# First loads of the attention stage moved into the last projection batch, queries stored in pieces there, output weights rounded one round later

## The chip, the cores and the metric

The kernel runs on one core of a Trainium2 chip. The metric is the device time of one execution in microseconds (us): the kernel before took 1955.43 us as the median of 3 runs, between 1955.02 and 1957.78. All times inside an execution come from one profiled execution. TensorE is called PE below, VectorE DVE, ScalarE ACT, GpSimd POOL; SP is the sync engine, which here only issues DMAs.

## The reference

Eight sequences of 512 tokens with 512 features go through one block: cross attention (16 heads of 32 features, with an additive bias for each head and a mask for each sequence) and a feed-forward part with a routed low-rank branch. Cut to what matters here:

```
q = split(layernorm(x) @ Wq.T + bq);  k = split(ctx @ Wk.T + bk);  v = split(ctx @ Wv.T + bv)
scores = q @ k^T / sqrt(32)
scores = where(mask == 0, -1e9, scores) + attn_bias          # bias: 16 heads x 512 x 512
probs = softmax(scores);  x = x + (probs @ v) @ Wo.T + bo
x = x + gelu(z @ W1.T) @ W2.T + routed low-rank term of z,   z = layernorm(x)
```

Everything is float32. Products that need it are made from a high and a low part of each operand ("rounding" a weight below means making these two parts).

## The kernel before, in words

The program has three blocks that follow each other, with a barrier of all engines between them; the first, `project`, ends only when all its DMAs to DRAM have landed.

`project` walks over the 8 sequences (batches). For each it computes keys, values and queries, in this order, and stores them to DRAM (`k_d`, `v_d`, `q_d`), with the mask turned into an additive array `pos_d`. Beside that it loads, splits and stores an eighth of the feed-forward weights (`load_ff`, `store_ff`, to `wf_d`). All DMAs of this block are issued by SP in program order, each behind the wait that stands before it. In a batch: `load_ff`, next context and x, store of the keys, store of `pos`, next mask, four stores of the values, one store of the queries (1 MB, after DVE has written the fourth query tile, L353), then `store_ff` (four DMAs of 512 KB).

`attend` has 8 rounds. A round is one group of 4 heads with 4 sequences: 16 steps, called quads here (a quad is 128 query rows of one sequence, with 4 heads; 128 quads in all, 16 in a round, counted from 0). For each head of a quad:
- PE multiplies queries by keys into PSUM (L651);
- POOL writes `pos - bias` into the buffer `t_s` (L619, 128x512). There are four buffers, so POOL may be up to four quads ahead. Six of the 64 tiles in a round are made by DVE instead (L727);
- DVE adds the two and takes the row minimum (L742); ACT takes the exponential (L797); PE turns the tile (L662), ACT and DVE copy it out (L784, L749), and PE multiplies by the values (L676).

At the start SP loads, for the first sequence, `pos`, queries, keys and values (`load_pos`, `load_qk`, `load_v`, 2.75 MB with the first bias rows), then waits for the fourth bias DMA before it goes on with the other three sequences. POOL issues the bias rows: `bias_t` holds four parts of 1 MB, for query rows `qt` 0 to 3; part 0 at once, parts 1 to 3 after the first queries and keys are there. Every second round POOL issues the next head group's four bias parts, one after each of its last four quads.

The output weights `Wo` are loaded in the first round and rounded there: ACT makes the high part at step `GQ` of round 0 (quad 4, L807), DVE the low part at step `GQ + 2` (quad 6, L773).

`blend` then does the output projection and the feed-forward part, and is the longest block.

## Time and profile before

| | |
|---|---|
| median of 3 runs | 1955.43 us |
| the profiled execution, its own time | 1953.16 us |
| its span, from first to last instruction | 1951.4 us |
| granted PE clock, mean | 0.979 of full |
| busy: PE, DVE, ACT, POOL | 1829.2, 1034.6, 794.3, 885.4 us |
| `project` | 0 to 318.3 us |
| `attend` | 318.9 to 935.8 us |
| `blend` | the rest |

The profile gives for each engine how long it was busy, and for a wait how long the engine sat idle and what ended that. The span is divided by the two barriers into the three blocks; a block has its own bound, and an average over the span says little on any of them. PE counts as busy while matmuls are in its pipeline.

### The profile page before, as it was taken

Reading aid. Unit: us, or ns where it says so; the run is one execution under the profiler, and the core shown is the slowest. Engines: PE = TensorE matmul, PEld = TensorE weight load, DVE = VectorE, ACT = ScalarE, POOL = GpSimd, SP = SyncE. Lnnn points to the kernel's source line nnn. Section 1 sums busy time; section 2 is a strip of 40 time slices with the busy share of each in tenths; the row PEclk is TensorE's granted clock in tenths of the full one; section 3 lists DMA queues with packets and bytes.
Section 4 is the critical chain, followed back from the end, with each engine's and each line's share of the span. In section 5 each row is a group of like instructions: output and inputs, shape, how many; then the busy total and the mean of one; then the engine's idle time right before and its main releaser. Section 6 shows DMA issues by size and latency. Waiting matters only on the chain.

```text
span 1951.4 us, 31562 instructions
## 1 busy us (share of the span) xinstructions
PE 1829.2 (94%) x11736; PEld 1363.2 (70%) x11736; DVE 1034.6 (53%) x2402; ACT 794.3 (41%) x1720; POOL 885.4 (45%) x705
## 2 busy tenths in 40 slices
...
GB/s 285 257 304 301 268 292 215 255 109 196 131 108 190 138 107 179 150 120 12 147 100 108 152 183 130 172 181 154 183 130 175 181 161 173 130 183 179 137 193 117
DMA packets 196359, 335.91 MB, mean 172 GB/s; under 512 B 10352, under 2 KB 51952, under 8 KB 196208
## 3 DMA queue, kind: packets, MB, share of 16 engines
...
q14 instruction: 55, 0.45, 0.1%
...
## 4 chain that ended last, share of the span: by engine, by line
PE 41%; DVE 5%; ACT 4%; issue 1%; DVEq 0%; POOL 0%; ACTq 0%
PE n_ps_h L1379 15%; PE n_ps_y L1398 14%; PE n_ps_m L1315 9%; PE n_ps_y L1315 2%; PE n_ps_m L1309 1%; DVE n_w L1087 1%; ACT n_g_f L1269 1%; DVE n_sel L1096 1%; DVE n_hl L1110 1%; ACT L1269 1%; ACT L1253 1%; ACT L1250 1%; DVE n_w L1091 1%; DVE n_w L1084 0%; ACT n_u L1250 0%
## 5 line engine op out<-in xcount | busy, mean ns | idle before, releaser
L619 POOL TENSOR_TENSOR a_t_s<-a_pos,a_bias_t 128x512 f32<-128x512 f32 x464 | 576.1, 1275 | 3.4 <-PE a_ps_t L662 3.1
L996 POOL TENSOR_TENSOR n_g_l<-n_g_f,n_g_h 128x512 fp32r<-128x512 f32 x128 | 184.3, 1440 | 676.4 <-DVE n_g_h L1169 676.4
L797 ACT ACTIVATE a_t_s<-a_t_s,a_nmax 128x512 f32<-128x512 f32 x512 | 364.3, 715 | 36.2 <-DVE a_nmax L742 36.0
L1379 PE MATMUL n_ps_h<-n_zT_h,n_w 128*128 128x512 f32 x1024 | 343.4, 397 | 2.1 <-DVE n_r_row L1145 2.1
L742 DVE CUSTOM_DVE_ANT_0 a_t_s<-a_ps_s,a_t_s 128x512 f32<-128x512 f32 x464 | 294.0, 687 | 64.1 <-PE a_ps_s L651 30.7
L1169 DVE CAST n_g_h<-n_g_f 128x512 fp32r<-128x512 f32 x128 | 54.6, 427 | 514.4 <-ACT n_g_f L1269 514.4
L662 PEld LDWEIGHTS a_ps_t<-ident,a_t_s 128*128 128x128 f32 x2048 | 222.0, 142 | 142.8 <-issue 108.8
L1398 PE MATMUL n_ps_y<-n_w,n_g_h 128*128 128x512 f32 x1024 | 316.2, 390 | 0.0
L1269 ACT ACTIVATE n_g_f<-n_ps_h 128x512 f32<-128x512 f32 x128 | 75.6, 596 | 547.3 <-PE n_ps_h L1379 547.3
L662 PE MATMUL a_ps_t<-ident,a_t_s 128*128 128x128 f32 x2048 | 282.4, 282 | 6.1 <-ACT a_pT L784 6.1
L1379 PEld LDWEIGHTS n_ps_h<-n_zT_h,n_w 128*128 128x128 f32 x1024 | 196.0, 191 | 43.3 <-DVE n_r_row L1145 2.5
L1398 PEld LDWEIGHTS n_ps_y<-n_w,n_g_h 128*128 128x128 f32 x1024 | 191.8, 188 | 39.4
L1379 PE MATMUL n_ps_h<-n_zT_l,n_w 128*128 128x512 f32 x512 | 202.4, 395 | 0.0
L1398 PE MATMUL n_ps_y<-n_w,n_g_l 128*128 128x512 f32 x512 | 199.5, 390 | 0.0
L784 ACT ACTIVATE a_pT<-a_ps_t 128x512 f32<-128x512 f32 x256 | 151.5, 592 | 74.0 <-PE a_ps_t L662 73.9
L651 PE MATMUL a_ps_s<-a_k,a_q 32*128 32x512 f32 x1024 | 148.4, 649 | 31.3 <-DMA a_k<-k_d 19.9
L749 DVE COPY a_pT<-a_ps_t 128x512 f32<-128x512 f32 x256 | 164.5, 683 | 7.0 <-PE a_ps_t L662 7.0
L676 PE MATMUL a_ps_o<-a_pT,a_v 128*32 128x256 f32 x2048 | 150.8, 390 | 0.0
L282 POOL TENSOR_TENSOR p_wf_l<-p_wf,p_wf_h 128x2048 fp32r<-128x2048 f32 x8 | 37.0, 4622 | 185.4 <-ACT p_wf_h L393 185.4
L1379 PEld LDWEIGHTS n_ps_h<-n_zT_l,n_w 128*128 128x128 f32 x512 | 98.1, 192 | 20.1
L1398 PEld LDWEIGHTS n_ps_y<-n_w,n_g_l 128*128 128x128 f32 x512 | 96.1, 188 | 19.9
L651 PEld LDWEIGHTS a_ps_s<-a_k,a_q 32*128 32x128 f32 x1024 | 41.4, 186 | 87.7 <-DVE a_nmax L742 46.9
...
## 6 DMA issues: line engine op xcount, KB each, us to landing
n_w<-wf_d SPq DMA_DIRECT2D x256, 512.0 KB, 4.0
a_pos<-pos_d SPq DMA_DIRECT2D x32, 1024.0 KB, 5.9
a_bias_t<-in_bias POOLq DMA_DIRECT2D x16, 1024.0 KB, 6.7
p_c_raw<-in_ctxT SPq DMA_DIRECT2D x8, 1024.0 KB, 7.5
p_x_raw<-in_x SPq DMA_DIRECT2D x8, 1024.0 KB, 9.7
p_m_raw<-in_mask SPq DMA_DIRECT2D x8, 1024.0 KB, 12.1
k_d<-p_k_s SPq DMA_DIRECT2D x8, 1024.0 KB, 11.6
pos_d<-p_pos SPq DMA_DIRECT2D x8, 1024.0 KB, 9.9
```

The source lines that it names most:

```text
L619: pool.tensor_tensor(out=t_s[:, j % NN, i, :], in0=pos[:, b, qt, :], in1=bias_t[:, i, qt, :], op=ALU.subtract).then_inc(nbm_pool, 1)
L651: pe.matmul(ps_s[:, i, :], q[rows, b, qt * P:(qt + 1) * P], k[rows, b, :], start=True, stop=True).then_inc(scored, 1)
L662: last = pe.transpose(ps_t[:, BANK[i], kt * P:(kt + 1) * P], t_s[:, at[1] % NN, i, kt * P:(kt + 1) * P], ident[:, :])
L676: last = pe.matmul(ps_o[rows, :], v[:, b, kt, rows], pT[:, h, i, kt, :], start=kt == 0, stop=kt == NT - 1)
L742: dve.tensor_tensor_reduce(t_s[:, j % NN, i, :], ps_s[:, i, :], added, 1.0, 3.0e38, ALU.add, ALU.min, nmax[:, j % NN, i:i + 1]).then_inc(s ...
L749: dve.tensor_copy(dst, src).then_inc(kept_dve, 1)
L784: act.activation(dst, src, ACT.Copy).then_inc(kept_act, 1)
L797: act.activation(t_s[:, j % NN, i, :], t_s[:, j % NN, i, :], ACT.Exp, scale=-1.0, bias=nmax[:, j % NN, i:i + 1], accum_out=total[:, j // 2 ...
L996: pool.tensor_tensor(out=g_l[:, f % NG, :], in0=g_f[:, f % NG, :], in1=g_h[:, f % NG, :].bitcast(F32), op=ALU.subtract).then_inc(g_low, 1)
L1315: last = pe.matmul(dst, stationary, moving, start=start and n == 0, stop=stop and n == len(passes) - 1)
L1379: last = pe.matmul(ps_h[:, f % 2, :], stationary, moving, start=i == 0, stop=i == len(passes) - 1)
L1398: last = pe.matmul(ps_y[:, t, :], gs[i], w2[:, f % NW, j, :], start=f == 0 and m == 0 and isinstance(b, int) and b == 0, stop=f == NF - 1 ...
```

## The change

It does four things.

1. Queries and keys of the first four sequences (`q`, `k`), the first sequence's `pos` and bias part 0 get their own SBUF space (`Ahead`) outside the blocks. In the last projection batch, behind `load_ff`, SP loads them there (`load_ahead`, ten DMAs, 4 MB). `attend` starts with them in place: SP then issues only `v` and `pos`, and POOL issues bias parts 1 to 3 with no wait between.
2. In the last batch the queries are stored in four pieces, each as soon as DVE has written its tile, with `store_ff` between the second and the third.
3. `Wo` is rounded at steps `GQ` and `GQ + 2` of round 1 instead of round 0.
4. `blend` takes the space of `Ahead` for its tiles `g_f`, `rc`, `hl`, `sel`, `u`, `w` and `ln_w`.

Its core:

```diff
+            def load_ahead():
+                sp.wait_ge(pos_out, 16 * 2)
+                sp.dma_start(ahead.pos[:, :, :], tokens(pos_d[0])).then_inc(ahead.pos_in, 16)
+                sp.dma_start(ahead.bias[:, :, :], bias[0, 0:HG, 0:P, :].rearrange("h p n -> p h n")) \
+                    .then_inc(ahead.bias_in, 16)
+                sp.wait_ge(q_out, 16 * (NT + 1))
+                sp.wait_ge(k_out, 16 * (NT + 1))
+                for n in range(NT):
+                    sp.dma_start(ahead.q[:, n, :], q_d[n]).then_inc(ahead.qk_in[n], 16)
+                    sp.dma_start(ahead.k[:, n, :], k_d[n]).then_inc(ahead.qk_in[n], 16)
             def body(b, more):
                 sp.wait_ge(wf_low, b + 1)
                 load_ff(b)
+                if not more:
+                    load_ahead()
...
-                sp.wait_ge(bank_free, NPB + NVQ * (b + 1))
-                store_qk(b, q_s, q_d, q_out)
-                sp.wait_ge(wf_low, b + 2)
-                store_ff(b)
+                if more:
+                    sp.wait_ge(bank_free, NPB + NVQ * (b + 1))
+                    store_qk(b, q_s, q_d, q_out)
+                else:
+                    for c in range(NC):
+                        if c == NC // 2:
+                            sp.wait_ge(wf_low, b + 2)
+                            store_ff(b)
+                        sp.wait_ge(bank_free, NPB + NVQ * b + NT + c + 1)
+                        sp.dma_start(q_d[B * c + b], q_s[:, c, :]).then_inc(q_out, 16)
+                if more:
+                    sp.wait_ge(wf_low, b + 2)
+                    store_ff(b)
...
-            load_pos(0, 0)
-            load_qk(0, 0)
             load_v(0, 0)
+            load_pos(0, 1)
+            load_v(0, 1)
             sp.wait_ge(bias_in[NT - 1], 16)
-            for j in range(1, NG):
+            for j in range(2, NG):
                 load_pos(0, j)
-                load_qk(0, j)
                 load_v(0, j)
...
-            load_bias(0, 0)
-            pool.wait_ge(qk_in[0], 32)
             for qt in range(1, NT):
                 load_bias(0, qt)
...
-                if isinstance(g, int) and g == 0 and j == GQ + 2:
+                if g == 1 and j == GQ + 2:
                     dve.wait_ge(kept.wo_high, 1)
...
-                if isinstance(g, int) and g == 0 and j == GQ:
+                if g == 1 and j == GQ:
                     act.wait_ge(kept.wo_in, 16)
...
-        g_f = sb("g_f", [P, NG, S])
+        g_f = ahead.pos
...
-        rc, hl, sel = sb("rc", [P, NT, NB]), sb("hl", [P, NT, NB]), sb("sel", [P, NT, NB])
-        u, w, ln_w = sb("u", [P, NT, NB]), sb("w", [P, NT, NB]), sb("ln_w", [P, NT, NB])
+        rc, hl, sel, u, w, ln_w = (a[:, n:n + 2, :].rearrange("p a (b n) -> p (a b) n", n=NB)
+                                   for a in (ahead.q, ahead.k, ahead.bias) for n in (0, 2))
```

SP's rows of the last projection batch, before (`p_wf` are the feed-forward weights as loaded, `p_wf_h` and `p_wf_l` their two parts; a DMA row ends with its shape):

```order
124 L216 DMA p_wf<-in_W1T 128x4x128
125 L218 DMA p_wf<-in_W2T 128x512
126 L212 DMA k_d<-p_k_s 128x4x512 [waits p_k_done]
127 L236 DMA pos_d<-p_pos 128x4x512 [waits p_pos_done]
128 L241 DMA v_d<-p_v_s 128x4x128 [waits p_bank_free]
129 L241 DMA v_d<-p_v_s 128x4x128 x3
130 L212 DMA q_d<-p_q_s 128x4x512 [waits p_bank_free]
131 L222 DMA wf_d<-p_wf_h 128x1024 [waits p_wf_low]
132 L223 DMA wf_d<-p_wf_l 128x1024
133 L222 DMA wf_d<-p_wf_h 128x1024
134 L223 DMA wf_d<-p_wf_l 128x1024
```

and the same place in the changed kernel, from the last row of `load_ff` to the keys' store (`h_` names are those of `Ahead`), and then from the values' store on:

```order
125 L232 DMA p_wf<-in_W2T 128x512
126 L241 DMA h_pos<-pos_d 128x4x512 [waits p_pos_out]
127 L242 DMA h_bias<-in_bias 128x4x512
128 L247 DMA h_q<-q_d 128x512 [waits p_k_out,p_q_out]
129 L248 DMA h_k<-k_d 128x512
134 L247 DMA h_q<-q_d 128x512
135 L248 DMA h_k<-k_d 128x512
136 L226 DMA k_d<-p_k_s 128x4x512 [waits p_k_done]
```

```order
139 L268 DMA v_d<-p_v_s 128x4x128 x3
140 L278 DMA q_d<-p_q_s 128x512 [waits p_bank_free] x2
141 L236 DMA wf_d<-p_wf_h 128x1024 [waits p_wf_low]
142 L237 DMA wf_d<-p_wf_l 128x1024
143 L236 DMA wf_d<-p_wf_h 128x1024
144 L237 DMA wf_d<-p_wf_l 128x1024
145 L278 DMA q_d<-p_q_s 128x512 [waits p_bank_free] x2
```

Ten loads now stand between `load_ff` and the store of the keys (rows 130 to 133 are two more pairs of `h_q` and `h_k`), and half of the queries leaves before `store_ff`, half behind it.

POOL's rows at the start of `attend`, before (`a_bias_t` is the bias, `a_t_s` what POOL writes):

```order
29 L606 DMA a_bias_t<-in_bias 128x4x512
30 L606 DMA a_bias_t<-in_bias 128x4x512 [waits a_qk_in0]
31 L606 DMA a_bias_t<-in_bias 128x4x512 x2
32 L619 TENSOR_TENSOR a_t_s<-a_pos,a_bias_t 128x512 [waits a_turned,a_bias_in0,a_pos_in0]
33 L619 TENSOR_TENSOR a_t_s<-a_pos,a_bias_t 128x512 [waits a_turned] x3
34 L619 TENSOR_TENSOR a_t_s<-a_pos,a_bias_t 128x512 [waits a_turned,a_bias_in1]
```

and in the changed kernel:

```order
29 L656 DMA a_bias_t<-in_bias 128x4x512 x3
30 L669 TENSOR_TENSOR a_t_s<-h_pos,h_bias 128x512 [waits a_turned,h_bias_in,h_pos_in]
31 L669 TENSOR_TENSOR a_t_s<-h_pos,h_bias 128x512 [waits a_turned] x3
32 L669 TENSOR_TENSOR a_t_s<-h_pos,a_bias_t 128x512 [waits a_turned,a_bias_in1]
33 L669 TENSOR_TENSOR a_t_s<-h_pos,a_bias_t 128x512 [waits a_turned] x2
```

One bias DMA and the wait for the first queries and keys are gone ahead of POOL's first tile; the tile's own shape is as it was.

## Rows read from the trace of the kernel before

**Rows 1.** Busy time by window around the last projection batch (columns as headed).

```profile
core 0: us, PE busy (x) PEld busy (x) DVE busy (x) ACT busy (x) POOL busy (x), PEclk, DMA share, GB/s
272.70:292.70 20.00, 19.32 (x94) 16.07 (x93) 13.11 (x27) 4.82 (x8) 1.01 (x1) 1.00 0.90 315
292.70:297.10 4.40, 4.40 (x26) 3.78 (x25) 1.39 (x2) 0.00 (x0) 0.00 (x0) 1.00 0.00 0
297.10:302.20 5.10, 5.10 (x25) 4.21 (x24) 0.75 (x1) 2.40 (x2) 2.43 (x1) 1.00 0.73 206
302.20:309.00 6.80, 5.96 (x27) 4.61 (x25) 2.25 (x3) 0.00 (x0) 2.18 (x1) 1.00 0.00 0
309.00:318.30 9.30, 0.00 (x0) 0.00 (x0) 0.00 (x0) 0.00 (x0) 0.00 (x0) 0.60 0.87 338
```

**Rows 2.** SP's DMA issues by time: start, duration, tile, count.

```profile
312.30 1.27 SPq L223 DMA_DIRECT2D wf_d<-p_wf_l  x1
...
318.91 0.37 SPq L542 DMA_DIRECT2D a_pos<-pos_d  x1
```

**Rows 3.** POOL by time: start, duration, count, idle time before and its releaser.

```profile
319.31 0.92 POOL L606 DMA_DIRECT2D a_bias_t<-in_bias  x1 [14.93 <-POOLq L119]
328.31 2.23 POOL L606 DMA_DIRECT2D a_bias_t<-in_bias  x3 [8.08 <-DMA a_k<-k_d]
330.56 39.40 POOL L619 TENSOR_TENSOR a_t_s<-a_pos,a_bias_t 128x512 f32<-128x512 f32 x32
...
374.43 6.49 POOL L619 TENSOR_TENSOR a_t_s<-a_pos,a_bias_t 128x512 f32<-128x512 f32 x4 [0.49 <-PE a_ps_t L662]
...
779.33 4.98 POOL L619 TENSOR_TENSOR a_t_s<-a_pos,a_bias_t 128x512 f32<-128x512 f32 x4
```

**Rows 4.** DVE by time, the same columns.

```profile
332.01 0.69 DVE L742 CUSTOM_DVE_ANT_0 a_t_s<-a_ps_s,a_t_s 128x512 f32<-128x512 f32 x1 [23.06 <-POOL a_t_s L619]
...
373.75 2.33 DVE L773 TENSOR_TENSOR k_wo_l<-k_az,k_wo_h 128x2048 fp32r<-128x2048 f32 x1
...
785.75 0.69 DVE L742 CUSTOM_DVE_ANT_0 a_t_s<-a_ps_s,a_t_s 128x512 f32<-128x512 f32 x1
```

**Rows 5.** ACT by time, at quad 4.

```profile
361.64 1.91 ACT L807 ACTIVATE k_wo_h<-k_az 128x2048 fp32r<-128x2048 f32 x1 [4.80 <-DMA k_az<-in_WoT]
```

**Rows 6.** PE by time, quads 0, 5, 8, 9 and 12 (L651).

```profile
328.06 2.09 PE L651 MATMUL a_ps_s<-a_k,a_q 32*128 32x512 f32 x8 [19.89 <-DMA a_k<-k_d]
...
355.44 1.14 PE L651 MATMUL a_ps_s<-a_k,a_q 32*128 32x512 f32 x8
...
379.62 1.14 PE L651 MATMUL a_ps_s<-a_k,a_q 32*128 32x512 f32 x8
...
383.87 1.14 PE L651 MATMUL a_ps_s<-a_k,a_q 32*128 32x512 f32 x8
...
398.01 1.14 PE L651 MATMUL a_ps_s<-a_k,a_q 32*128 32x512 f32 x8
```

**Rows 7.** The page's group of POOL's tiles: busy, mean ns, idle before, releaser.

```profile
L619 POOL TENSOR_TENSOR a_t_s<-a_pos,a_bias_t 128x512 f32<-128x512 f32 x464 | 576.1, 1275 | 3.4 <-PE a_ps_t L662 3.1
```

**Rows 8.** Waits in 318 to 930: total us, times, longest us.

```profile
DVE a_t_s L742 <- POOL a_t_s L619: 27.3, 13, 23.1
```

**Rows 9.** Busy time by window at the start of `attend` (columns as in rows 1).

```profile
322.00:326.00 4.00, 0.00 (x0) 0.00 (x0) 0.00 (x0) 0.00 (x0) 0.00 (x0) 0.50 1.00 373
...
334.00:338.00 4.00, 1.58 (x8) 0.52 (x8) 1.40 (x4) 2.40 (x6) 4.00 (x5) 0.50 1.04 394
```

**Rows 10.** DMA issues one by one: KB, us from issue to landing.

```profile
q_d<-p_q_s SPq DMA_DIRECT2D x1, 1024.0 KB, 4.2
...
wf_d<-p_wf_l SPq DMA_DIRECT2D x1, 512.0 KB, 6.0
...
a_pos<-pos_d SPq DMA_DIRECT2D x1, 1024.0 KB, 5.7
a_bias_t<-in_bias POOLq DMA_DIRECT2D x1, 1024.0 KB, 9.5
```

More of the change, by code:

```diff
@@ L56, in build, with __init__, sb @@
         neg_half = top.enter_context(nc.sbuf_tensor("neg_half", [P, NT], F32))
+        ahead = Ahead(nc, top)
         project(nc, ident, ones, neg_half, x, ctxT, mask, WqT, bq, WkT, bk, WvT, bv, W1T, W2T,
-                q_d, k_d, v_d, pos_d, wf_d)
+                q_d, k_d, v_d, pos_d, wf_d, bias, ahead)
         kept = Kept(nc, top)
-        attend(nc, ident, bias, q_d, k_d, v_d, pos_d, att_d, x, WoT, bo, rawU, rawV, kept)
-        blend(nc, ident, ones, neg_half, x, att_d, ln_g, ln_b, rWT, rb, gamma, wf_d, kept, out)
+        attend(nc, ident, bias, q_d, k_d, v_d, pos_d, att_d, x, WoT, bo, rawU, rawV, kept, ahead)
+        blend(nc, ident, ones, neg_half, x, att_d, ln_g, ln_b, rWT, rb, gamma, wf_d, kept, ahead, out)
+class Ahead:
+    def __init__(self, nc, stack):
+        def sb(name, shape):
+            return stack.enter_context(nc.sbuf_tensor("h_" + name, shape, F32))
+        self.q, self.k = sb("q", [P, NT, S]), sb("k", [P, NT, S])
+        self.pos = sb("pos", [P, NT, S])
+        self.bias = sb("bias", [P, HG, S])
+        self.qk_in = [stack.enter_context(nc.semaphore(f"h_qk_in{n}")) for n in range(NT)]
+        self.pos_in, self.bias_in = (stack.enter_context(nc.semaphore("h_" + n)) for n in ("pos_in", "bias_in"))
 class Kept:
@@ L114, in project @@
 def project(nc, ident, ones, neg_half, x, ctxT, mask, WqT, bq, WkT, bk, WvT, bv, W1T, W2T,
-            q_d, k_d, v_d, pos_d, wf_d):
+            q_d, k_d, v_d, pos_d, wf_d, bias, ahead):
     NPJ = 3 * NC
@@ L259, in _ @@
             sp.wait_ge(k_out, 16 * (B + 1))
-            sp.wait_ge(q_out, 16 * (B + 1))
+            sp.wait_ge(q_out, 16 * (B + NC))
             sp.wait_ge(v_out, 16 * NC * (B + 1))
@@ L449, in _, with attend @@
             walk(pe, body)
-def attend(nc, ident, bias, q_d, k_d, v_d, pos_d, att_d, x, WoT, bo, rawU, rawV, kept):
+def attend(nc, ident, bias, q_d, k_d, v_d, pos_d, att_d, x, WoT, bo, rawU, rawV, kept, ahead):
     NG = 4
@@ L471, in sem @@
             return ctx.enter_context(nc.semaphore("a_" + name))
-        q, k = sb("q", [P, NG, S]), sb("k", [P, NG, S])
+        q, k = ahead.q, ahead.k
         v = sb("v", [P, NG, NT, P])
-        pos = sb("pos", [P, NG, NT, S])
-        bias_t = sb("bias_t", [P, HG, NT, S])
+        pos_more = sb("pos", [P, NG - 1, NT, S])
+        bias_more = sb("bias_t", [P, HG, NT - 1, S])
         t_s = sb("t_s", [P, NN, HG, S])
@@ L487, in attend @@
         ps_o = ctx.enter_context(nc.psum_tensor("a_ps_o", [P, HALF], F32))
-        qk_in = [sem(f"qk_in{n}") for n in range(NG)]
+        qk_in = ahead.qk_in
         v_in = [sem(f"v_in{n}") for n in range(NG)]
-        pos_in = [sem(f"pos_in{n}") for n in range(NG)]
+        pos_in = [ahead.pos_in] + [sem(f"pos_in{n}") for n in range(1, NG)]
         bias_in = [sem(f"bias_in{t}") for t in range(NT)]
@@ L499, in attend, with pos_rows, bias_rows, wait_bias @@
         passed = sem("passed")
+        def pos_rows(j, qt, end):
+            return ahead.pos[:, qt:end, :] if j == 0 else pos_more[:, j - 1, qt:end, :]
+        def bias_rows(i, end, qt):
+            return ahead.bias[:, i:end, :] if qt == 0 else bias_more[:, i:end, qt - 1, :]
+        def wait_bias(eng, hg, qt):
+            if qt == 0 and hg == 0:
+                eng.wait_ge(ahead.bias_in, 16)
+            else:
+                eng.wait_ge(bias_in[qt], 16 * (hg + (qt > 0)))
         def lagged(g, j, lag):
@@ L541, in load_pos @@
             def load_pos(g, j):
-                sp.dma_start(pos[:, j, :, :], tokens(pos_d[g % (B // NG) * NG + j])).then_inc(pos_in[j], 16)
+                sp.dma_start(pos_rows(j, 0, NT), tokens(pos_d[g % (B // NG) * NG + j])).then_inc(pos_in[j], 16)
             def load_qk(g, j):
@@ L605, in load_bias @@
                 rows = slice(qt * P, (qt + 1) * P)
-                pool.dma_start(bias_t[:, :, qt, :], bias[0, hg * HG:(hg + 1) * HG, rows, :].rearrange("h p n -> p h n")) \
+                pool.dma_start(bias_rows(0, HG, qt), bias[0, hg * HG:(hg + 1) * HG, rows, :].rearrange("h p n -> p h n")) \
                     .then_inc(bias_in[qt], 16)
```

17 lines of the change are left out of this document (8 added, 9 removed).

## The prediction, made before the result was known

> **What bounds the kernel now.** I read the windows first, since the change sits at one barrier. The last projection batch runs from about 272 us, and SP's queue has holes in it: DMA share 0.90, then 0.00 for 4.4 us, 0.73 while the values leave, 0.00 for 6.8 us, and then 0.87 for 9.3 us in which no engine computes [rows 1]. That last stretch is the store of the queries and of the feed-forward weights: the last DMA is issued at 312.30 and lands 6.0 us later, at 318.3 [rows 2, 10]. `attend` starts at 318.91 with its loads [rows 2].
>
> Then the queues by time. PE sits idle for 19.89 us, until the first keys are there at 328.06 [rows 6]; only then POOL issues three bias DMAs, 2.23 us, and starts its first tile at 330.56. DVE starts at 332.01, after 23.06 us idle, released by POOL [rows 3, 4]. So the first tile of `attend` hangs on POOL, and POOL on the first keys.
>
> What bounds the rest of `attend` decides what an earlier start is worth. Two chains run side by side. POOL's 464 tiles are busy 576.1 us and idle only 3.4, 3.1 of it for PE [rows 7]: POOL practically never stops. But DVE waits for POOL only 13 times, 27.3 us in all, 23.1 of it at the start [rows 8]: behind the start POOL is nearly always ahead, and the chain PE-DVE-ACT sets the pace. So there are two limits close together. How close, I read at the worst place, the first quad of the last head group (quad 96), just behind POOL's four bias issues: POOL's four tiles end at 779.33 + 4.98 = 784.31 [rows 3], and DVE takes the fourth of them at 785.75 [rows 4]. POOL's lead is down to 1.4 us there. POOL loses time to bias issues at the end of each head group and makes it up on the way; behind quad 96 it loses none any more.
>
> The stall that the third edit is about: in round 0 ACT waits 4.80 us for `Wo` and computes 1.91 us [rows 5], and DVE spends 2.33 us [rows 4]. Quads 5 to 8 start 24.18 us apart, quads 9 to 12, the same three steps undisturbed, 14.14 [rows 6]. The chain loses 10.0 us. POOL hardly does: it runs through with 32 tiles in 39.40 us [rows 3].
>
> **The change part by part.** *End of `project`.* Ten loads, 4 MB (4.19 million bytes), join SP's queue. At the full pace of loads, 373 to 394 GB/s [rows 9], they take 10.6 to 11.2 us; I take 10.8. They stand behind `load_ff`, and what comes later in the queue (keys, `pos`, values, queries, `store_ff`) is pushed back into the holes, which are 4.4 + 6.8 = 11.2 us [rows 1]. Nobody waits for those stores before the barrier. Where the queue no longer runs dry, its two restarts go as well: a lone 1 MB store takes 4.2 us to land [rows 10] for 2.7 us of transfer at that pace, 1.5 us each time, 3.0 for two. So the queue ends earlier by 11.2 + 3.0 - 10.8 = 3.4 us, at 314.9. Bounds: the bytes of 272.7 to 318.3 (20 us at 315, 5.1 at 206, 9.3 at 338 GB/s: 10.5 million) plus 4.2 make 14.7; at 338 GB/s from 272.7 they end at 316.2, 2.1 us earlier than now. On the other side the fourth query piece cannot be issued before 309.0 [rows 1], and with the 6.0 us of a DMA in a full queue [rows 10] it lands at 315.0, or at 313.2 with the 4.2 of a lone one: at best 5.1 us. The splitting of the queries alone has no term: they share the queue with `store_ff`, whose wait, for POOL's 4.6 us on the weights, is over early in the window of 302.2 to 309.0: POOL is busy 2.18 us of it [rows 1].
>
> *Start of `attend`.* SP and POOL begin 0.6 us behind the landing, at 315.5 and 315.9. POOL issues its three bias DMAs (2.23 us) and starts its first tile at 315.9 + 2.25 = 318.15, where it stood at 330.56: 12.4 us earlier. Of this 3.4 is the queue's and 9.0 the wait for `q` and `k`. DVE follows 1.45 us later, as now (332.01 - 330.56). The first tile's data are there by then: `pos`, bias, `q` and `k` stand in the queue ahead of seven stores that must land before the barrier.
>
> *What is late next:* bias part 1. POOL needs it for its fifth tile, 4 x 1.24 us (39.40 / 32) behind the first, at 323.1. Now a bias part issued together with SP's loads takes 9.5 us, while SP's `pos` of the same size takes 5.7 [rows 10]. It landed when nearly all of the 2.75 MB was through; in the changed kernel 2.5 MB are ahead of or beside it, so 9.5 x 2.5 / 2.75 = 8.6 us, at 324.5. POOL stalls 1.4 us. Bounds: 0 (with 5.7) and 2.3 (with 9.5). Parts 2 and 3 follow at 2.7 us each, faster than the 3.7 to 5 us in which POOL uses one up.
>
> The Trainium skill says otherwise on that wait: by "DMA: Bandwidth & Descriptors", section "Queues, rings and completion order", each DMA engine takes turns between its queues packet by packet. Two equal transfers would then end together; the rows have 5.7 and 9.5 us, so here the measurement decides. By the rule part 1 would be there after about 7.7 us, at 323.6, and the stall would be 0.5 instead of 1.4.
>
> *`Wo` one round later.* The wait of 4.80 us goes, since `Wo` is loaded long before; 1.91 us on ACT and 2.33 on DVE stay, in round 1. The chain gains 10.0 less between 0 and 4.2; I take 3.3 (all of DVE's, as the nearer engine to the limit, and half of ACT's): 6.7. POOL gains its idle time for PE, 3.1 us [rows 7], since the chain is no longer four quads behind. One loss stays POOL's in both kernels: beside DVE's 2.33 us four tiles took 6.49 instead of 4.98 [rows 3], 1.5 us.
>
> "SBUF — State Buffer" of the Trainium skill, section "Who interferes with whom", lets a DVE operation with two SBUF inputs block POOL for its whole length. The rows show 1.5 of 2.33 us; if the new place made it all of it, POOL would lose 0.8 us more.
>
> *`blend`'s tiles and the views of `pos` and bias* change addresses, not shapes: nothing, bounded by nothing that a row shows.
>
> **The sum.** The chain alone would end `attend` 12.4 + 6.7 = 19.1 us earlier. But POOL must have quad 96's tiles ready: 784.31 - 330.56 - 3.1 = 450.65 us of POOL's work behind its first tile, so at 318.15 + 1.4 + 450.65 = 770.2. DVE can take the fourth at 770.2 instead of 785.75: 15.5 us earlier. It is the smaller of the two, and behind quad 96 the chain keeps its pace. So 12.4 (start) + 3.1 (POOL's waits) + 1.4 (its lead) - 1.4 (bias part 1) = 15.5 us. `blend` shifts by it whole. From the profiled execution's 1953.16 us that leaves 1937.7; the median of the runs is 2.3 us above that execution, and I predict 1940 us as the next median.
>
> **The rivals.** *A: the chain is the limit to the end*, because POOL makes up the missing 4 us (its idle time was more than the profile shows, or bias part 1 is in time). For it: DVE waits for POOL 4.2 us in all behind the start [rows 8]. Against it: 464 tiles at 1.24 us leave POOL no reserve. Gain 17 (POOL without the stall) to 19: 1937.
>
> *B: the queue does not end earlier.* The 4 MB only just fit the holes. If loads and stores mixed run at 315 GB/s (the mean of the first window [rows 1]), 14.7 million bytes take 46.7 us, to 319.4: 1.1 later than now. With the full 2.3 us stall the gain is 15.5 - 4.5 - 0.9 = 10: 1945.
>
> *C: no change.* The transfers were hidden behind something the profile does not name, for instance code that must be loaded at the barrier; or POOL's tiles beside more DMA traffic take longer. Then only what the chain can use is left, under 4 us: 1953.
>
> *D: slower.* The queue is the place: everything in `project` must land before the barrier, and ten loads are put ahead of it. Its price is set by the pace of the mixed queue. At 206 GB/s, the pace while the values leave [rows 1], 14.7 million bytes take 71 us, to 344: 26 us later than now, against which stand 9.0 + 3.1 + 1.4 - 1.4 = 12: 14 us slower, 1969. It decides at 318.3 + 12.1 = 330.4, 57.7 us of transfer or 255 GB/s. Against it: the first window holds 315, and the 206 is mostly the restart of a queue with 1 MB in it.
>
> **How the numbers follow.** Under 0.2%, 3.9 us, a measurement cannot tell this kernel from no change. Chances: the forecast 0.45, A 0.22, B 0.23, C 0.06, D 0.04. Faster by more than 0.2% are the first three, 0.90; within it 0.06; slower 0.04. The range takes in A with the queue at its best bound (15.5 + 1.7 + 1.4, and a little of the chain's) and B: 1935 to 1946.
>
> **What the profile after would show.** Right: the windows from 287 to 309 us with a DMA share near 0.9; the last landing at 313 to 316; PE's first scores within 1 us of the barrier, POOL's first tile 2.7 us behind it; one POOL wait of 1 to 2 us before its fifth tile; no ACT wait for `Wo`, and PE's quads 5 to 8 in 14 us; DVE waits for POOL late in each head group, more than now; and POOL's tiles without a gap. Wrong: a last landing behind 318 (B or D), DVE that still never waits for POOL (A), POOL tiles over 1.3 us, or a `blend` that is longer than before.

## The result and the profile after

| | before | after |
|---|---|---|
| median | 1955.43 us (13 runs, 1952.08 to 1959.76) | 1948.85 us (13 runs, 1943.87 to 1950.81) |
| ratio, with its 95% interval | | 0.9961 [0.9952, 0.9969] |
| profiled execution, its span | 1951.4 us | 1947.8 us |
| first scores of `attend` (PE) | 328.06 us | 317.06 us |
| scores of the last quad (127) | 925.01 us | 919.14 us |

The changed kernel is faster, by 6.6 us in the medians. The forecast was 15.5 us less than before, 1940 us, with a range to 1946: the sign was right, the size was not, and the time lies outside the range.

The two profiled executions must be set against each other with care: in that of after, `project` runs 2.2 us late from its first 60 us on, before any instruction that the change touches (its last batch starts at 274.90 instead of 272.70). In the kernels below this shift is between nothing and 2.1 us (e3 2.0, e6 1.7, e7 1.8, e4 0.2), so I compare durations between two points of one execution where I can, and raw times where the shift does not matter.

The windows around the last projection batch, the same columns as in [rows 1] and the stretches 2 to 3 us later, with a sixth window from round 1 of `attend`:

```profile
274.90:294.90 20.00, 19.32 (x94) 16.01 (x93) 13.14 (x27) 4.81 (x8) 1.01 (x1) 1.00 0.99 344
294.90:299.30 4.40, 4.40 (x26) 3.78 (x24) 1.33 (x2) 0.00 (x0) 0.00 (x0) 1.00 1.05 387
299.30:305.00 5.70, 5.70 (x27) 4.73 (x27) 0.81 (x2) 2.40 (x2) 2.97 (x1) 1.00 1.06 396
305.00:311.00 6.00, 5.43 (x24) 4.15 (x23) 2.03 (x3) 0.00 (x0) 1.65 (x1) 1.00 1.09 397
311.00:316.30 5.30, 0.00 (x0) 0.00 (x0) 0.22 (x1) 0.00 (x0) 0.00 (x0) 0.83 0.70 279
427.00:441.00 14.00, 4.10 (x40) 2.19 (x32) 14.00 (x12) 3.93 (x11) 11.76 (x10) 0.75 0.00 1
```

The holes of [rows 1] are full: share 0.00, 0.73 and 0.00 became 1.05, 1.06 and 1.09, at 387 to 397 GB/s. The stretch in which no engine computes has shrunk from 9.3 to 5.3 us. The sixth window is the trouble: DVE busy for 14 us of 14, and no DMA at all.

SP's issues by time (start, duration, tile, count), the last pieces of the queries and the first load of `attend`, against [rows 2]:

```profile
309.71 2.44 SPq L278 DMA_DIRECT2D q_d<-p_q_s  x2
317.01 0.37 SPq L600 DMA_DIRECT2D a_v<-v_d  x1
```

POOL by time (start, duration, count, idle time before and its releaser), against [rows 3]:

```profile
317.40 2.42 POOL L656 DMA_DIRECT2D a_bias_t<-in_bias  x3 [10.75 <-POOLq L133]
319.83 4.93 POOL L669 TENSOR_TENSOR a_t_s<-h_pos,h_bias 128x512 f32<-128x512 f32 x4
326.25 6.19 POOL L669 TENSOR_TENSOR a_t_s<-h_pos,a_bias_t 128x512 f32<-128x512 f32 x5 [1.48 <-DMA a_bias_t<-in_bias]
...
427.69 4.97 POOL L669 TENSOR_TENSOR a_t_s<-a_pos,h_bias 128x512 f32<-128x512 f32 x4
432.63 6.13 POOL L669 TENSOR_TENSOR a_t_s<-a_pos,a_bias_t 128x512 f32<-128x512 f32 x5
443.88 2.50 POOL L669 TENSOR_TENSOR a_t_s<-a_pos,a_bias_t 128x512 f32<-128x512 f32 x2 [5.12 <-PE a_ps_t L710]
...
773.44 4.98 POOL L669 TENSOR_TENSOR a_t_s<-h_pos,h_bias 128x512 f32<-128x512 f32 x4
```

The first tile stands at 319.83 instead of 330.56, and the one wait for bias part 1 is there, 1.48 us. At 438.76 POOL has no buffer left and waits 5.12 us for PE.

DVE by time, against [rows 4]:

```profile
321.29 0.69 DVE L789 CUSTOM_DVE_ANT_0 a_t_s<-a_ps_s,a_t_s 128x512 f32<-128x512 f32 x1 [10.07 <-POOL a_t_s L669]
...
430.06 10.85 DVE L820 TENSOR_TENSOR k_wo_l<-k_az,k_wo_h 128x2048 fp32r<-128x2048 f32 x1
440.83 0.68 DVE L789 CUSTOM_DVE_ANT_0 a_t_s<-a_ps_s,a_t_s 128x512 f32<-128x512 f32 x1
...
779.88 0.69 DVE L789 CUSTOM_DVE_ANT_0 a_t_s<-a_ps_s,a_t_s 128x512 f32<-128x512 f32 x1
```

The line of 10.85 us decides the case. The same operation on the same tile, the low part of `Wo`, took 2.33 us before [rows 4] and takes 10.85 now. Everything behind it on DVE waits, and then PE does.

PE by time, quads 0, 5 and 8, then 23 and 24 with what PE does just ahead of 24, against [rows 6]:

```profile
317.06 2.09 PE L699 MATMUL a_ps_s<-h_k,h_q 32*128 32x512 f32 x8 [6.63 <-PEq L133]
...
345.65 1.14 PE L699 MATMUL a_ps_s<-h_k,h_q 32*128 32x512 f32 x8
...
359.78 1.14 PE L699 MATMUL a_ps_s<-h_k,h_q 32*128 32x512 f32 x8
...
428.93 1.14 PE L699 MATMUL a_ps_s<-h_k,h_q 32*128 32x512 f32 x8
...
441.67 1.08 PE L733 MATMUL a_ps_s<-ident,a_rinv 128*32 128x128 f32 x16 [10.57 <-DVE a_nmax L789]
...
446.44 1.71 PE L699 MATMUL a_ps_s<-h_k,h_q 32*128 32x512 f32 x8
```

Quads 5 to 8 are 14.13 us apart, where they were 24.18. Quads 23 and 24 are 17.51 apart, where they were 4.96; PE has idled 10.57 us for DVE, and its granted clock was 0.50 of full (1.2 GHz) from 441 to 446 us and 1.00 again from 452 on (in the kernel before it was 1.00 from 436 to 460). Set against the scores of before, PE is 11.0 us earlier at quad 0, 19.84 from quad 8 to 21, 6.44 at quad 24 (452.88 before), and 5.87 from quad 25 to the end. The gain was there and went in one step.

ACT at the high part of `Wo`, against [rows 5]: no wait is left.

```profile
420.21 1.91 ACT L854 ACTIVATE k_wo_h<-k_az 128x2048 fp32r<-128x2048 f32 x1
```

The waits from 318 to 930 us (engine, what it waited for: total us, times, longest), against [rows 7, 8]:

```profile
DVE a_t_s L789 <- POOL a_t_s L669: 14.1, 12, 10.1
...
POOL a_t_s L669 <- PE a_ps_t L710: 8.1, 3, 5.1
...
POOL a_t_s L669 <- DMA a_bias_t<-in_bias: 1.5, 1, 1.5
```

POOL's waits for PE were to vanish from 3.1 us; they are 8.1 (5.12, 2.45 and 0.56), all behind DVE's long operation.

### The profile page after: what moved, and what is told of

Read it like the earlier page. It is cut to its first block, busy times and chain, and to the rows that moved or that the text cites. A ratio compares the mean times of both kernels' runs of the same rounds, so it can differ in the third digit from the quotient of the medians.

```text
span 1947.8 us, 31566 instructions
## 1 busy us (share of the span) xinstructions
PE 1834.0 (94%) x11736; PEld 1365.9 (70%) x11736; DVE 1043.5 (54%) x2402; ACT 794.6 (41%) x1720; POOL 882.9 (45%) x704
## 4 chain that ended last, share of the span: by engine, by line
PE 42%; DVE 5%; ACT 4%; issue 1%; DVEq 0%; POOL 0%; ACTq 0%
PE n_ps_h L1426 15%; PE n_ps_y L1445 14%; PE n_ps_m L1362 9%; PE n_ps_y L1362 2%; PE n_ps_m L1356 1%; DVE h_bias L1134 1%; ACT h_pos L1316 1%; DVE h_k L1143 1%; DVE h_q L1157 1%; ACT L1316 1%; ACT L1300 1%; ACT L1297 1%; DVE h_bias L1138 1%; DVE h_bias L1131 0%; ACT h_k L1297 0%
## 5 line engine op out<-in xcount | busy, mean ns | idle before, releaser
L1043 POOL TENSOR_TENSOR n_g_l<-h_pos,n_g_h 128x512 fp32r<-128x512 f32 x128 | 184.2, 1439 | 680.9 <-DVE n_g_h L1216 680.9
L1216 DVE CAST n_g_h<-h_pos 128x512 fp32r<-128x512 f32 x128 | 54.6, 426 | 516.3 <-ACT h_pos L1316 516.3
L669 POOL TENSOR_TENSOR a_t_s<-a_pos,a_bias_t 128x512 f32<-128x512 f32 x256 | 317.7, 1271 | 7.8 <-PE a_ps_t L710 7.6
L1316 ACT ACTIVATE h_pos<-n_ps_h 128x512 f32<-128x512 f32 x128 | 75.6, 596 | 548.2 <-PE n_ps_h L1426 548.1
L699 PE MATMUL a_ps_s<-h_k,h_q 32*128 32x512 f32 x1024 | 148.4, 649 | 18.9 <-DVE a_nmax L789 8.4
L669 POOL TENSOR_TENSOR a_t_s<-a_pos,h_bias 128x512 f32<-128x512 f32 x96 | 119.6, 1270 | 0.6 <-PE a_ps_t L710 0.6
```

Of the source, the lines that this page charges most:

```text
L669: pool.tensor_tensor(out=t_s[:, j % NN, i:i + 1, :], in0=pos_rows(b, qt, qt + 1), in1=bias_rows(i, i + 1, qt), op=ALU.subtract).then_inc(n ...
L699: pe.matmul(ps_s[:, i, :], q[rows, b, qt * P:(qt + 1) * P], k[rows, b, :], start=True, stop=True).then_inc(scored, 1)
L1043: pool.tensor_tensor(out=g_l[:, f % NG, :], in0=g_f[:, f % NG, :], in1=g_h[:, f % NG, :].bitcast(F32), op=ALU.subtract).then_inc(g_low, 1)
```

## The experiments

All of them were timed against the kernel before, whose medians beside them were 1955.44 to 1956.28 us; each experiment has 4 to 12 executions. One of the twelve of e2_only_wo_round1 took 2330.37 us, the others 1952.91 to 1965.78, and its median counts all twelve. The next table gathers them; "from scores to scores" is the time from the first scores of `attend` to those of quad 127 in the profiled execution, which is free of the shift in `project`; the low part is the time of the operation (or the piece of it) that the row moves.

| kernel | median us | ratio [95%] | first scores | quad 127 | from scores to scores | low part of `Wo` |
|---|---|---|---|---|---|---|
| before | 1955.43 | 1 | 328.06 | 925.01 | 596.95 | DVE 2.33 |
| after | 1948.85 | 0.9961 [0.9952, 0.9969] | 317.06 | 919.14 | 602.08 | DVE 10.85 |
| e1_wo_round0 | 1948.21 | 0.9961 [0.9946, 0.9976] | 317.04 | 920.57 | 603.53 | DVE 12.33 |
| e2_only_wo_round1 | 1959.96 | 1.0013 [1.0, 1.0026] | 328.59 | 927.81 | 599.22 | DVE 10.11 |
| e3_wo_low_pool_end | 1938.35 | 0.9907 [0.9891, 0.9923] | 316.89 | 909.54 | 592.65 | POOL 4.55 |
| e4_reduce_in_place | 1939.01 | 0.9911 [0.9896, 0.9926] | 315.10 | 908.43 | 593.33 | as e3 |
| e5_pool_pause | 1942.89 | 0.994 [0.9928, 0.9953] | 316.12 | 914.63 | 598.51 | DVE 2.28 |
| e6_bias_first | 1935.22 | 0.9893 [0.988, 0.9907] | 316.75 | 907.48 | 590.73 | as e3 |
| e7_no_pieces | 1942.53 | 0.9939 [0.9926, 0.9951] | 320.80 | 913.29 | 592.49 | as e3 |
| e8_low_in_pieces | 1944.73 | 0.9945 [0.9931, 0.9958] | 314.75 | 914.65 | 599.90 | DVE 9.28 (first quarter) |
| e9_seventh_tile | 1938.82 | 0.9911 [0.9895, 0.9926] | 316.33 | 909.66 | 593.33 | as e3 |

The rest of the program, from quad 127's scores on, takes 1025.4 to 1030.4 us in these profiled executions, 1026.4 in that of before and 1028.7 in that of after. The change touches it only by the addresses of `blend`'s tiles (its part 4), e3 and its successors by when the first attention output is loaded. Kernels with the same `blend` differ by as much as before and after do, so the 2.3 us between these two are not shown to be the change's; why it varies was not tried.

The theory: DVE's subtraction of `Wo` reads two tiles in SBUF, as nothing else that DVE does at this place (the tiles that it takes over from POOL are no exception: there DVE subtracts the bias from the scores where they lie, in PSUM); while POOL's tiles run one behind the other, it does not get on, and it ends only when POOL stops. The first rival: the place in round 1 is at fault (a transfer, the PE clock, the order around quad 22), and in round 0 the operation would take its 2.33 us. The second: the operation is long and dear in itself wherever DVE has it.

**e1_wo_round0** puts the rounding back to round 0 of the changed kernel.

```diff
-                if g == 1 and j == GQ + 2:
+                if g == 0 and j == GQ + 2:
...
-                if g == 1 and j == GQ:
+                if g == 0 and j == GQ:
```

> The changed kernel with Wo rounded in round 0 again (part 3 of the change undone). Theory 1: DVE's low part of Wo (two SBUF inputs) cannot start while POOL's tiles run back to back; it gets its turn only when POOL pauses, and POOL pauses only when it is four quads ahead. At quad 6 POOL is 1 to 3 quads ahead, so the operation should again take 8 to 13 us instead of 2.33, and the time be 1947 to 1951 us, as the changed kernel's. Theory 2: the operation is slow only where the change put it (round 1: other addresses, other neighbours); back in round 0 it takes 2.3 us as in the kernel before, and the time is 1940 to 1944 us.

DVE by time, at the low part of `Wo`:

```profile
356.95 12.33 DVE L820 TENSOR_TENSOR k_wo_l<-k_az,k_wo_h 128x2048 fp32r<-128x2048 f32 x1
```

POOL by time, beside it (the four tiles ahead of these are unbroken as well):

```profile
360.93 6.20 POOL L669 TENSOR_TENSOR a_t_s<-a_pos,a_bias_t 128x512 f32<-128x512 f32 x5
372.24 2.51 POOL L669 TENSOR_TENSOR a_t_s<-a_pos,a_bias_t 128x512 f32<-128x512 f32 x2 [5.11 <-PE a_ps_t L710]
```

POOL stops at 367.13, its tiles at 1.24 us each as ever, and DVE's operation ends at 369.28, 2.15 us later, about what it takes alone (2.28 us in e5 below). In the changed kernel the same difference is 440.91 - 438.76 = 2.15. It is not the round. The medians cannot tell this kernel from the changed one (1948.21 and 1948.85; from scores to scores it is 1.5 us longer): moving the rounding to round 1 is worth nothing that can be measured, for with the earlier loads ACT's wait of 4.80 us [rows 5] is gone in round 0 as well.

**e2_only_wo_round1** is the kernel before with the third part of the change alone.

```diff
-                if isinstance(g, int) and g == 0 and j == GQ + 2:
+                if g == 1 and j == GQ + 2:
...
-                if isinstance(g, int) and g == 0 and j == GQ:
+                if g == 1 and j == GQ:
```

> The kernel before with only part 3 of the change. Theory 1: without the wait for Wo in round 0 POOL's lead stays small, it never pauses, and the low part in round 1 takes 8 to 13 us; the 10 us won in round 0 are given back: 1953 to 1957 us, no change. Theory 2 in the form that the start of the attention stage (loads, buffers of Ahead) is the cause: the operation takes 2.3 us here, and the time is 1948 to 1950 us.

DVE by time:

```profile
440.40 10.11 DVE L773 TENSOR_TENSOR k_wo_l<-k_az,k_wo_h 128x2048 fp32r<-128x2048 f32 x1
```

POOL by time:

```profile
434.84 13.51 POOL L619 TENSOR_TENSOR a_t_s<-a_pos,a_bias_t 128x512 f32<-128x512 f32 x11
453.47 2.51 POOL L619 TENSOR_TENSOR a_t_s<-a_pos,a_bias_t 128x512 f32<-128x512 f32 x2 [5.12 <-PE a_ps_t L662]
```

Without the early loads it is the same: POOL stops at 448.35, DVE ends at 450.51, 2.16 us behind. The chain is 9.49 us ahead of before until quad 21, by the wait that goes, and 2.8 us behind it from quad 24. This part alone brings nothing or costs a little (1.0013 [1.0, 1.0026]).

Why was it cheap before? There POOL was about to stop, by chance. POOL and DVE by time in the kernel before, around 373.75 us:

```profile
370.17 3.77 POOL L619 TENSOR_TENSOR a_t_s<-a_pos,a_bias_t 128x512 f32<-128x512 f32 x3 [0.21 <-PE a_ps_t L662]
373.75 2.33 DVE L773 TENSOR_TENSOR k_wo_l<-k_az,k_wo_h 128x2048 fp32r<-128x2048 f32 x1
374.43 2.78 POOL L619 TENSOR_TENSOR a_t_s<-a_pos,a_bias_t 128x512 f32<-128x512 f32 x1 [0.49 <-PE a_ps_t L662]
```

The 4.80 us wait on ACT had put the chain so far behind that POOL ran out of buffers. DVE's operation started in the last of POOL's tiles, which ended at 373.94, and ended at 376.08, 2.14 us behind it: the same distance as in the other kernels. POOL's pause of 0.49 us let it in, and POOL's next tile took 2.78 us instead of 1.24 and ended 1.13 us behind DVE's end: this time POOL waited, for all that was left of DVE's operation. The stall that the change removes was what made the operation cheap.

**e3_wo_low_pool_end** takes the operation off DVE: POOL does it behind its last tile, where nobody waits for POOL. SP's load that needs it moves ahead of the last store.

```diff
             for j in range(NG):
+                if j == NG - 1:
+                    sp.wait_ge(kept.wo_low, 1)
...
+            pool.wait_ge(kept.wo_high, 1)
+            pool.tensor_tensor(out=kept.wo[1][:, :, :], in0=kept.az[:, :, :],
+                               in1=kept.wo[0][:, :, :].bitcast(F32), op=ALU.subtract).then_inc(kept.wo_low, 1)
...
-                if g == 1 and j == GQ + 2:
-                    dve.wait_ge(kept.wo_high, 1)
-                    dve.tensor_tensor(out=kept.wo[1][:, :, :], in0=kept.az[:, :, :],
-                                      in1=kept.wo[0][:, :, :].bitcast(F32), op=ALU.subtract).then_inc(kept.wo_low, 1)
```

> The changed kernel with the low part of Wo made by POOL behind its last tile of the attention stage instead of by DVE in round 1 (SP then loads the first attention output behind that). Theory 1: DVE is never held; the chain keeps its 19.8 us until POOL's lead becomes the limit, so the gain is that of POOL's start and lead, 13 to 15 us in the profile: 1940 to 1943 us. Theory 3 (the stall in round 1 only took the place of one that POOL's lead would have caused anyway): 1946 to 1950 us. POOL's own operation is expected at 4.6 us.

POOL by time: the start, quad 96, and the moved operation.

```profile
319.67 4.93 POOL L671 TENSOR_TENSOR a_t_s<-h_pos,h_bias 128x512 f32<-128x512 f32 x4
326.34 3.73 POOL L671 TENSOR_TENSOR a_t_s<-h_pos,a_bias_t 128x512 f32<-128x512 f32 x3 [1.75 <-DMA a_bias_t<-in_bias]
...
765.42 4.98 POOL L671 TENSOR_TENSOR a_t_s<-h_pos,h_bias 128x512 f32<-128x512 f32 x4
...
908.99 4.55 POOL L686 TENSOR_TENSOR k_wo_l<-k_az,k_wo_h 128x2048 fp32r<-128x2048 f32 x1
```

DVE by time, the third and fourth tile of quad 96:

```profile
769.35 0.69 DVE L794 CUSTOM_DVE_ANT_0 a_t_s<-a_ps_s,a_t_s 128x512 f32<-128x512 f32 x1 [0.53 <-issue]
770.58 0.69 DVE L794 CUSTOM_DVE_ANT_0 a_t_s<-a_ps_s,a_t_s 128x512 f32<-128x512 f32 x1 [0.54 <-issue]
```

The kernel is 17.1 us faster than before, two and a half times the gain of the change. Here the forecast's picture can be seen. The chain is ahead of before by 19.75 us behind round 0, and then by 18.9 at quad 24, 18.07 at quad 63, 16.58 at quad 95, 15.12 at quad 98, and 15.47 at quad 127: the gain is cut down at each new head group, behind POOL's bias issues. At quad 96 POOL's fourth tile ends at 765.42 + 4.98 = 770.40, and DVE takes it at 770.58. The lead of 1.4 us is 0.2, and the limit is POOL.

**e4_reduce_in_place** asks whether any DVE operation at that place is held. It is e3 with a reduction of the same 128x2048 tile put where the subtraction was; it reads one tile in SBUF, not two, and writes only 128x4. It adds an operation whose result is not used.

```diff
+                if g == 1 and j == GQ + 2:
+                    dve.wait_ge(kept.wo_in, 16)
+                    dve.tensor_reduce(junk[:, :], kept.az[:, :, :], AX_X, ALU.min).then_inc(junk_done, 1)
```

> As e3, with one more operation: at the place where DVE made the low part (round 1, quad 22) DVE takes a minimum over Wo, as long (2.3 us) but with one SBUF input and a 128x4 output. Theory 1 (it is the second SBUF input): it takes 2.3 us although POOL runs on, and the time is 0 to 2.5 us above e3. If any long DVE operation is held there: 8 to 13 us, and 1948 us or more.

DVE by time:

```profile
429.12 2.28 DVE L827 TENSOR_REDUCE a_junk<-k_az 128x4 f32<-128x2048 f32 x1
```

POOL by time:

```profile
430.87 12.47 POOL L673 TENSOR_TENSOR a_t_s<-a_pos,a_bias_t 128x512 f32<-128x512 f32 x10
```

2.28 us, with POOL's tiles at 1.25 us beside it: neither holds the other. So it is not the length of the operation nor the place. The reduction differs from the subtraction in its small output too, but a large output in SBUF is not what holds DVE either: its most frequent operation reads one tile in PSUM and one in SBUF and writes 128x512 to SBUF, beside the same POOL tiles, and in the changed kernel none of its 464 took more than 0.693 us:

```profile
L789 DVE CUSTOM_DVE_ANT_0 a_t_s<-a_ps_s,a_t_s 128x512 f32<-128x512 f32 x464 | 294.2, 687 | 52.6 <-PE a_ps_s L699 31.6
```

What is left as the difference is the second SBUF input. The quad is 2.9 us late there (435.85 - 427.99 = 7.86 us instead of 4.96), and the kernel as a whole is as fast as e3, which loses about as much later on to POOL: e4 is 16.6 us ahead of before from quad 25 to the end, with no loss at the head groups.

**e5_pool_pause** leaves the subtraction on DVE and has POOL wait for it.

```diff
+                if g == 1 and j == 2 * GQ:
+                    pool.wait_ge(kept.wo_low, 1)
```

> The changed kernel, with POOL made to wait before its first tile of quad 24 until DVE has written the low part of Wo. Theory 1 (POOL's unbroken run holds DVE's operation, and nothing else does): POOL stands still when DVE comes to it, the operation takes 2.3 us instead of 10.85, the chain loses 2 to 3 us there instead of 13, and POOL waits about 4.7 us; POOL is then the limit at the head-group ends, and the gain over the changed kernel is 3 to 5 us: 1943 to 1946 us. If something else held the operation: 10 us again and 1949 to 1954 us.

DVE by time:

```profile
430.15 2.28 DVE L822 TENSOR_TENSOR k_wo_l<-k_az,k_wo_h 128x2048 fp32r<-128x2048 f32 x1
```

POOL by time:

```profile
432.56 4.99 POOL L671 TENSOR_TENSOR a_t_s<-a_pos,h_bias 128x512 f32<-128x512 f32 x4 [5.53 <-issue]
```

With POOL still the operation takes 2.28 us, at the same place with the same two inputs. That shows it from the other side. POOL's 5.53 idle us come back at the end, as they must where POOL is the limit: 598.51 from scores to scores, 5.86 more than e3.

**e6_bias_first** is e3, and SP waits for bias part 1 before it issues the second `pos` and what follows.

```diff
             load_v(0, 0)
+            sp.wait_ge(bias_in[1], 16)
             load_pos(0, 1)
```

> As e3 (low part on POOL at the end, 1938.35 us), with SP waiting for bias part 1 before it loads the second sequence's pos and v. If POOL's 1.5 us wait before its fifth tile comes from the shared transfers, part 1 lands about 5.5 us after its issue, the wait goes, and since POOL is the limit up to quad 96 all of it counts: 1 to 1.5 us less than e3, about 1937. If POOL's start is not what limits, no change.

POOL by time:

```profile
319.54 4.92 POOL L672 TENSOR_TENSOR a_t_s<-h_pos,h_bias 128x512 f32<-128x512 f32 x4
324.42 8.62 POOL L672 TENSOR_TENSOR a_t_s<-h_pos,a_bias_t 128x512 f32<-128x512 f32 x7
```

The stall of 1.75 us is gone, and `attend` is 1.9 us shorter from scores to scores (592.65 to 590.73): one for one, since POOL is the limit. This is the lowest median, 1935.22 us, though the interval of its ratio overlaps with that of e3.

**e7_no_pieces** is e3 with the last batch's queries stored whole, and the feed-forward weights behind them, as before.

```diff
-                    for c in range(NC):
-                        if c == NC // 2:
-                            sp.wait_ge(wf_low, b + 2)
-                            store_ff(b)
-                        sp.wait_ge(bank_free, NPB + NVQ * b + NT + c + 1)
-                        sp.dma_start(q_d[B * c + b], q_s[:, c, :]).then_inc(q_out, 16)
...
+                sp.wait_ge(bank_free, NPB + NVQ * (b + 1))
+                store_qk(b, q_s, q_d, q_out)
+                sp.wait_ge(wf_low, b + 2)
+                store_ff(b)
```

> As e3, with the last batch's queries stored in one piece after the fourth tile and store_ff behind it, as in the kernel before (part 2 of the change undone). If the queue is what ends the projection block: 1 MB of queries and 2 MB of weights are then issued from 309 us on and land at 318 to 320, 2 to 4 us later than in e3, all of it lost again by POOL's limit: 1940.5 to 1942.5 us. If the pieces do nothing: 1938.4.

SP's issues by time:

```profile
310.81 0.36 SPq L226 DMA_DIRECT2D q_d<-p_q_s  x1
...
320.75 0.37 SPq L591 DMA_DIRECT2D a_v<-v_d  x1
```

`attend` starts 3.9 us later (first scores 320.80 instead of 316.89), and 3.75 of it are still there at quad 127; the medians differ by 4.2. The queries' whole 1 MB and the 2 MB of feed-forward weights are issued from 310.81 on, where the changed kernel has two pieces of 256 KB left at 309.71. In e7 the last of the weights land at 320.11; with this execution's shift of 1.8 us taken out that is 318.3, as in the kernel before (318.28). Without the pieces the projection block ends no earlier at all.

**e8_low_in_pieces** leaves the low part on DVE, as four 128x512 pieces behind four quads.

```diff
-                if g == 1 and j == GQ + 2:
+                if g == 1 and GQ + 2 <= j < GQ + 2 + NC:
+                    c = j - GQ - 2
...
+                    dve.tensor_tensor(out=kept.wo[1][:, c, :], in0=kept.az[:, c, :],
+                                      in1=kept.wo[0][:, c, :].bitcast(F32), op=ALU.subtract).then_inc(kept.wo_low, 1)
```

> The changed kernel, with DVE's low part of Wo in four operations of 128x512 (0.6 us each) behind quads 22 to 25 instead of one of 128x2048. Theory 1: also a short operation has to wait for POOL's pause, so the first takes 8 to 11 us, and the others little if POOL is then still in its pause, or each up to 2 us; the time is again 1947 to 1951 us. Rival: the operation shares the port in turns with POOL and the hold grows with its length: each piece takes 2 to 3 us, and the chain hides part of it: 1943 to 1946 us.

DVE by time, the first piece:

```profile
427.88 9.28 DVE L821 TENSOR_TENSOR k_wo_l<-k_az,k_wo_h 128x512 fp32r<-128x512 f32 x1
```

POOL by time:

```profile
430.42 6.19 POOL L669 TENSOR_TENSOR a_t_s<-a_pos,a_bias_t 128x512 f32<-128x512 f32 x5
440.12 2.50 POOL L669 TENSOR_TENSOR a_t_s<-a_pos,a_bias_t 128x512 f32<-128x512 f32 x2 [3.52 <-PE a_ps_t L710]
```

A quarter of the data, and 9.28 us: POOL stops at 436.61, the piece ends at 437.16, 0.55 us behind. What is paid is the time until POOL's next stop, not the size. The later pieces, in a time in which POOL keeps pausing, take 0.74 to 1.47 us. The median is 4.1 us below that of the changed kernel, of which 2.2 us show from scores to scores; the two intervals overlap, and the rest is not explained.

**e9_seventh_tile** is e6 with one more of POOL's tiles in each round given to DVE, to take load off the engine that limits e6.

```diff
-    DVE_NBM = (1, 3, 5, 7, 9, 11)
+    DVE_NBM = (1, 3, 5, 6, 7, 9, 11)
```

> As e6 (1935.22 us), with DVE making one more of POOL's 64 tiles in each round (quad 6, fourth head). In e6 POOL is the limit at the ends of the head groups (DVE waits for it at quads 32, 64 and 96). One tile less is 1.24 us a round, so POOL falls out as a limit: up to quad 96 the chain gets back the 3 to 4 us that it lost at these places, less 0.7 to 1 us a round of DVE's own work where that is not hidden. If POOL's limit counts as described: 1931 to 1935 us. If DVE's extra work costs a full 0.7 to 1 us in each of the 8 rounds: 1937 to 1940 us.

The waits of POOL from 318 to 930 us:

```profile
POOL a_t_s L672 <- PE a_ps_t L716: 6.4, 9, 1.1
```

POOL now waits for PE, 6.4 us in all, where e6 shows none of it: the bound has moved to the chain, and the chain is 2.6 us longer than e6 (593.33 against 590.73). A miss: no gain, and in the profiled executions a loss, though the intervals of the two ratios overlap.

The times against what was expected: e1, e4 and, at its upper edge, e7 came out in the range that the theory gave. e3, e5 and e6 came out faster than theirs, e3 by 1.7 us, e5 by 0.1, and e6 gained 3.1 us on e3 where 1 to 1.5 were expected. e2's median lies 3 us above its range, its ratio is no change, as expected. e8's time lies below the 1947 to 1951 us of the theory and in the range of its rival, that each piece takes 2 to 3 us; the durations (9.28, 1.47, 0.74 and 1.00 us) are those of the theory. e9 fell into the range given for the case in which DVE's extra work costs its full time.

## Why the prediction was right in part and wrong in size

*The queue.* Right in size, by luck in part. The last landing is at 316.33; less the 2.2 us by which this execution's `project` is late, 314.1, where 314.9 was forecast. The mixed queue ran at 344 to 397 GB/s as long as it was full; B had it at 315, D below 255. But it is not the bytes that end the block: the last store of weights lands at 315.04, and the last landing is that of the fourth piece of the queries, issued at 311.25, once DVE has written its tile, and 5.1 us under way. That is the case which the prediction had as its other bound. And the pieces, of which it said "The splitting of the queries alone has no term", are all of this gain: without them the block ends where it did before (e7).

*Start of `attend`.* Right. POOL's first tile is 10.7 us earlier in raw time, 12.9 with the shift taken out; forecast 12.4. PE's first scores come 0.7 us behind the last landing.

*Bias part 1.* Right in size: a stall of 1.48 us (1.75 in e3), forecast 1.4. In the changed kernel its load took 8.8 us against 8.6 forecast, beside 7.8 for SP's `pos` of the same size, in the DMA issues one by one:

```profile
a_pos<-pos_d SPq DMA_DIRECT2D x1, 1024.0 KB, 7.8
...
a_bias_t<-in_bias POOLq DMA_DIRECT2D x1, 1024.0 KB, 8.8
```

The prediction's estimate from the turn-taking between queues of the Trainium skill's "DMA: Bandwidth & Descriptors", section "Queues, rings and completion order", was 7.7 us and a stall of 0.5. The two are now much closer than before (5.7 and 9.5 us, [rows 10]), but the row is nearer to my 8.6.

*POOL as the limit, and the sum of 15.5.* Right in mechanism, where it could show itself. In e3 `attend` starts 11.2 us earlier in raw time and is 4.3 us shorter from scores to scores: 15.47, or 17.5 with that execution's shift of 2.0 taken out. The medians have 17.1 (the interval of the ratio makes it 15.1 to 21.3). The sum must be changed in four places for e3: POOL no longer loses the 1.5 us beside DVE's operation [rows 3]; the start is 12.9 instead of 12.4 (319.67, less the shift of 2.0, against 330.56); the stall 1.75 instead of 1.4; and 0.2 of the lead stays. 15.5 + 1.5 + 0.5 - 0.35 - 0.2 = 17.0. POOL's waits for PE are gone there, as the sum had it.

*The step that failed* is in "`Wo` one round later": "1.91 us on ACT and 2.33 on DVE stay, in round 1", priced at 3.3 us for the chain. ACT's 1.91 stayed; DVE's 2.33 became 10.85, and the chain, 19.84 us ahead at quad 21, is 5.87 ahead from quad 25 on: 14.0 us, of which 0.8 are ACT's. I took the duration from one row in which POOL happened to stop, and the edit took away the reason of that stop. The prediction had the right pair in hand and looked at it from one side only: it asked what DVE's operation would do to POOL (0.8 us more), never what POOL's unbroken run of tiles would do to DVE's operation. It cost 12.6 us of chain between quads 23 and 24 alone, and 0.6 more at the next. That is more than the operation's 10.85; PE's clock, at 0.50 of full behind its idle time, is one reason that the rows show, and how much of the 2.3 us is its share was not tried.

The prediction also misread the row on the other side. It took 1.5 of DVE's 2.33 us as the part for which POOL is held, and left 0.8 open. POOL's tile was released 0.68 us behind DVE's start, and it took 1.54 us longer than another, of the 1.65 that were left of DVE's operation: nearly all of it, as the rule that it cited has it.

The section that the prediction cited, "Who interferes with whom" of the Trainium skill's "SBUF — State Buffer", has both sides: "Issue order, not op shape, decides who blocks." It also says that a DVE instruction with two SBUF inputs contends with a GpSimd instruction that reads SBUF, and that a reduction never does on trn2; the changed kernel (10.85 us) and e4 (2.28 us beside POOL's tiles) agree. By that rule taken one instruction at a time DVE would have waited for the tile that POOL was in, 1.24 us at most. The runs show it held over all of POOL's tiles until its next pause: seven whole ones in the changed kernel, eight in e1.

Where the time went: quads 23 and 24 stand 17.51 us apart instead of 4.96 before, which is the 12.6 us. POOL, which was to set the end, was pulled along: it stood still for 5.12 us and 2.45 more. The chain is then the limit to the end: DVE takes quad 96's fourth tile at 779.88 and POOL had it ready at 773.44 + 4.98 = 778.42, 1.5 us earlier, the lead that it had before. So the 15.5 were cut to 5.87 in raw time, 8.0 with the shift; the medians say 6.6. (In the profiled executions the rest behind quad 127 takes 2.3 us of it back.)

*The rivals.* A (the chain is the limit to the end) describes what bounds the changed kernel, but for another reason and at another time; e3 shows that with the operation out of the way it is POOL. B and C did not happen. None of them had a held operation in it, and so the range ended too low.

*Of the things to look for*, the DMA shares, the landing, the first scores, the one POOL wait, ACT without a wait and quads 5 to 8 in 14 us came out. "POOL's tiles without a gap" did not, and DVE's late waits for POOL did not become more (4.0 us behind the start, 4.2 before). The first of these is the mark of the error. Of the signs of being wrong, a `blend` longer than before is there by 2.3 us, within what it varies by.

*The parts by themselves:* loading ahead with the queries in pieces is the whole gain; the pieces, tried in e3's kernel and not in the changed one, are worth 3.9 us there (e7); the rounding one round on is worth nothing (e1), or less alone (e2). The place of `blend`'s tiles was not tried alone.

Open: why `project` is up to 2.2 us late in some executions, and why the rest behind quad 127 varies by 5 us. No experiment was made on either.
